# Causal attention in fp32 by row groups, four heads at a time, in a block of state-space scan, attention and experts

## What is computed

```
h   = layernorm(x, ln1_g, ln1_b)
qkv = (h @ Wqkv).reshape(B, T, 16, 48)
q, k, v = qkv[..., :16], qkv[..., 16:32], qkv[..., 32:]
q, k = rope(q), rope(k)                      # T = 2048
scores = einsum("bqhd,bkhd->bhqk", q, k) / sqrt(16)
scores = where(causal, scores, -1e9)
attn = einsum("bhqk,bkhd->bqhd", softmax(scores), v).reshape(B, T, 256) @ Wproj
x = x + attn                                 # then layernorm, gates, experts
```

## Time and profile before

| | us |
|---|---|
| median of three runs | 4523.81 |
| lowest and highest | 4516.04, 4532.55 |
| the profiled execution | 4527.28 |
| its span, first to last instruction | 4525.8 |
| PE busy | 3529.3 (78%) |
| DVE busy | 2918.2 (64%) |
| ACT busy | 2646.1 (58%) |
| POOL busy | 1823.3 (40%) |

### The profile page before, as it was taken

The page is one execution under the profiler, slowest core; times in us unless marked ns, Lnnn a source line. Parts: engine busy times, 40 slices in busy tenths (PEclk is TensorE's granted clock), DMA queues, the critical chain, the costliest instruction groups (busy, mean ns, idle before and its releaser), DMA issues. The chain is left out here.

```text
span 4525.8 us, 71351 instructions
## 1 busy us (share of the span) xinstructions
PE 3529.3 (78%) x20742; PEld 2162.1 (48%) x20742; DVE 2918.2 (64%) x4398; ACT 2646.1 (58%) x4174; POOL 1823.3 (40%) x1644
## 2 busy tenths in 40 slices
PE   8478788878878877847776888888888884599990
...
GB/s 204 133 107 91 85 96 100 97 85 95 85 87 99 89 93 85 85 133 198 177 164 87 25 27 25 24 20 25 27 25 27 25 12 140 102 77 77 66 29 186
DMA packets 183457, 385.83 MB, mean 85 GB/s; under 512 B 21763, under 2 KB 96630, under 8 KB 168624
## 3 DMA queue, kind: packets, MB, share of 16 engines
...
## 5 line engine op out<-in xcount | busy, mean ns | idle before, releaser
L506 POOL TENSOR_TENSOR scan_hC<-scan_hh,scan_cbc 128x512 f32<-128x512 f32 x1024 | 1383.2, 1379 | 159.0 <-DVE scan_hh L718 101.0
L718 DVE TENSOR_TENSOR_SCAN scan_hh<-scan_dA,scan_state,scan_bx 128x512 f32<-128x512 f32 x1024 | 1253.3, 1265 | 212.4 <-PE scan_bx L810 96.0
L1456 DVE TENSOR_REDUCE attend_mx<-attend_s 128x1 f32<-128x512 f32 (+1 forms) x1360 | 782.0, 608 | 342.1 <-PE attend_s L1586 222.1
L810 PE MATMUL scan_bx<-kept_ident,scan_dBxT 128*128 128x128 f32 x4096 | 675.8, 291 | 197.5 <-DVE scan_hh L718 133.7
L559 ACT ACTIVATE scan_dBxT<-scan_dtxT,scan_bt 128x512 f32<-128x512 f32 x1028 | 655.6, 710 | 81.5 <-PE scan_bx L810 81.3
L820 PE MATMUL scan_acc<-kept_ident,scan_hC 128*128 128x128 f32 x4128 | 655.7, 286 | 56.6 <-ACT scan_uu L568 29.9
L810 PEld LDWEIGHTS scan_bx<-kept_ident,scan_dBxT 128*128 128x128 f32 x4096 | 501.3, 150 | 389.1 <-DVE scan_hh L718 233.2
L554 ACT ACTIVATE scan_dA<-scan_dt,scan_an 128x512 f32<-128x512 f32 x1028 | 660.9, 712 | 29.4 <-DVE scan_hh L718 29.3
L1550 ACT ACTIVATE attend_full<-attend_s 128x1024 f32<-128x1024 f32 x384 | 392.0, 1025 | 332.2 <-PE attend_s L1613 328.2
L1586 PE MATMUL attend_s<-attend_kt,attend_qt 96*128 96x512 bf16 (+1 forms) x1360 | 482.8, 373 | 131.3 <-DVE attend_mx L1456 72.8
L820 PEld LDWEIGHTS scan_acc<-kept_ident,scan_hC 128*128 128x128 f32 x4128 | 516.3, 149 | 71.7 <-POOL scan_hC L506 38.3
...
...
## 6 DMA issues: line engine op xcount, KB each, us to landing
...
```

Source lines behind the costliest of these rows:

```text
L506: pool.tensor_tensor(hC[n % 2][:, m, :], h[:, m, :], rows, ALU.mult).then_inc(hc_ok, 1)
L718: dve.tensor_tensor_scan(hh[n % 2][:, m, r], dA[n % 2][:, m, r], bx[bank(j)][:, r], state[:, d, n, m:m + 1], ALU.mult, ALU.add).then_inc(h ...
L810: last = pe.transpose(bx[bank(j)][:, t * P:(t + 1) * P], dBxT[turned_slot(n)][:, t, m * P:(m + 1) * P], k["ident"][:, :])
L1456: dve.tensor_reduce(mx[:, t, c:c + 1], s1[v % 2][:, 0:w], AX_X, ALU.max).then_inc(s1_read, 1)
```

## The change

Queries and keys stay fp32 and are no longer split. In mix, POOL makes the rotation's sums, PE turns `rot` in four items of 128 columns (eight heads of q or of k), ACT copies four tiles of 512 columns and stores each. The reciprocal roots are issued in the third item and after the fourth.

```diff
-                        low(j - 1, q - 1)
-                low(JT - 1, t * JT + JT - 1)
+                    rotate(j, t * JT + j, t)
                 pool.wait_ge(v_out, t * JT + JT)
                 hold(pool, k)
                 pool.dma_start(vav[b, c].rearrange("p j (h e) -> p j h e", h=H), vt[i][:, :, :, :]
@@ -1086,12 +1076,6 @@
                 dve.tensor_tensor(ht[:, :, :], ht[:, :, :], gb[:, 1:2, :].broadcast_to([P, JT, D]), ALU.add
...
-                spread_parts(JT - 1, t * JT + JT - 1)
-                for h in range(H):
-                    g = h // 4
-                    act.wait_ge(hd_turned, t * H + h + 1)
-                    if h % 4 == 0:
...
+                for it in range(ITEMS):
+                    act.wait_ge(hd_turned, t * ITEMS + it + 1)
+                    act.wait_ge(stored_h[it], t * 16)
+                    act.activation(hd[it][:, :], ph[it % 2][:, :], ACT.Copy).then_inc(hd_out, 1)
+                    if it:
+                        store_heads(b, c, t, it - 1)
+                    if it == ITEMS - 2:
+                        rstd_of(0, t + 1)
+                store_heads(b, c, t, ITEMS - 1)
...
-                pe.wait_ge(lo_ok, t * JT + JT + 1)
-                for h in range(H):
-                    pe.wait_ge(hd_out, t * H + h)
-                    for w in range(2):
...
+                pe.wait_ge(rot_ok, t * JT + JT + 2)
+                for it in range(ITEMS):
+                    w, half = it // KD, it % KD
+                    pe.wait_ge(hd_out, t * ITEMS + it)
+                    for j in range(JT):
+                        last = pe.transpose(ph[it % 2][:, j * P:(j + 1) * P],
+                                            rot[:, j, w, half * (H // 2):(half + 1) * (H // 2), :].rearrange(
+                                                "p h e -> p (h e)"), k["ident"][:, :])
                     last.then_inc(hd_turned, 1)
```

```diff
+    HG = 4
+    GROUPS = B * H // HG
+    SETS = 3
+    PB = 3
+    HALF = C // 2
+    steps = [(qc, kt) for qc in range(NC) for kt in range(JT * qc + JT)]
+    NSTEP = len(steps)
+    N1 = HG * sum(t // JT + 1 for t in range(KT))
...
+    firsts = []
+    for t in range(KT - 1, -1, -1):
+        for c in range(t // JT + 1):
+            if t % JT == 0 and c == t // JT:
+                firsts[-1].append((t, c))
+            else:
+                firsts.append([(t, c)])
+    assert len(firsts) < NSTEP - 2
...
+            for n in range(GROUPS):
+                b, g = n // (H // HG), n % (H // HG)
+                for st, (qc, kt) in enumerate(steps):
+                    at = n * NSTEP + st
+                    if kt < JT * qc:
+                        continue
+                    o = (kt - JT * qc) * P
+                    pool.wait_ge(exp_ok, at * 2 + 2)
+                    own = pb[at % PB][:, :, o:o + P]
+                    pool.affine_select(out=own, in_=own, compare_op=ALU.is_ge, fill=0.0, base=0,
+                                       pattern=[[0, HG], [1, P]], channel_multiplier=-1).then_inc(kept_ok, 1)
+                    if st in ends:
+                        v = n * NC + qc
+                        pool.wait_ge(pv_out, v + 1)
+                        hold(pool, k)
...
+                for t, c, h in tiles1(st, (2, 3)) + tiles1(st, (0, 1)):
+                    bank = s1[v % S1]
+                    dve.wait_ge(s1_mm, v + 1)
+                    if c < t // JT:
+                        dve.tensor_reduce(mx[:, h, t, c:c + 1], bank[:, :], AX_X, ALU.max).then_inc(s1_read, 1)
+                    else:
+                        w = t % JT * P
+                        if w:
+                            dve.tensor_reduce(mx[:, h, t, c:c + 1], bank[:, 0:w], AX_X, ALU.max)
+                        if h == 2 and t < KT - 2:
+                            dve.wait_ge(edge_ok, n * KT + KT - 2 - t)
+                        dve.tensor_tensor(edge[t % 2][:, h, :], bank[:, w:w + P], cap_s[:, :], ALU.min
+                                          ).then_inc(s1_read, 1)
+                    v += 1
+                for t, c in firsts[st]:
+                    if c == t // JT:
+                        dve.wait_ge(s1_read, v)
+                        dve.tensor_reduce(mx[:, :, t, JT], edge[t % 2][:, :, :], AX_X, ALU.max).then_inc(edge_ok, 1)
...
+            for at in range(GROUPS * NSTEP):
+                qc, kt = steps[at % NSTEP]
+                o = max(kt - JT * qc, 0) * P
+                if at in outs:
+                    evacuate(outs[at])
+                if at >= PB:
+                    act.wait_ge(pv_ok, at - PB + 1)
+                for pair in range(2):
+                    act.wait_ge(s2_mm, at * 2 + pair + 1)
+                    own, score = pb[at % PB][:, 2 * pair:2 * pair + 2, :], s2[pair]
+                    if kt < JT * qc:
+                        act.activation(own, score[:, :, :], ACT.Exp).then_inc(exp_ok, 1)
                     else:
-                        for r in range(2):
-                            o = (2 * half + r) * P
-                            last = act.activation(buf[:, 2 * half + r, o:], s2[st % 2][:, r, o:], ACT.Exp)
-                    last.then_inc(s2_read, 1)
-                    if st - 2 in ends:
-                        evacuate(i, n, nth, ends.index(st - 2))
-                    if i == 1 and st - 1 in ADD_AT:
-                        invert(nth, ADD_AT[st - 1])
-                    if st == PLACE_AT:
-                        place_max((j + 2) % SETS, n + 2)
-                evacuate(i, n, nth, NC - 1)
-                if i == 1:
-                    invert(nth, NC - 1)
-            heads(act, head)
-            act.wait_ge(m_in, (B * H + 2) * 48)
+                        act.activation(below[pair][:, :, :], score[:, :, o:o + P], ACT.Relu, scale=-1.0
+                                       ).then_inc(clip_ok, 1)
+                        clips += 1
+                        if o + P < C:
+                            act.activation(own[:, :, o + P:], score[:, :, o + P:], ACT.Exp)
+                        act.wait_ge(clip_ok, clips)
+                        act.activation(own[:, :, o:o + P], below[pair][:, :, :], ACT.Exp, scale=-1.0
+                                       ).then_inc(exp_ok, 1)
+            evacuate(GROUPS * NC - 1)
...
+            def scores1(n, st, heads):
...
+                v = n * N1 + before1[st] + (0 if heads[0] == 2 else 2 * len(firsts[st]))
+                for t, c, h in tiles1(st, heads):
+                    rows = head_rows(h)
                     w = min(C, (t + 1) * P - c * C)
...
+                    if v >= S1:
+                        pe.wait_ge(s1_read, v - S1 + 1)
+                    pe.matmul(s1[v % S1][:, 0:w], qt[n % SETS][rows, t * P:(t + 1) * P],
+                              kt_[n % SETS][rows, c * C:c * C + w], start=True, stop=True).then_inc(s1_mm, 1)
+                    v += 1
...
+            def scores2(at, pair):
+                n, (qc, kt) = at // NSTEP, steps[at % NSTEP]
+                o = max(kt - JT * qc, 0) * P
+                if at % NSTEP == 0 and pair == 0:
+                    pe.wait_ge(m_in, (n + 1) * HG * 16)
+                if at:
+                    pe.wait_ge(exp_ok, at * 2 - 1 + pair)
...
+                    h = 2 * pair + i
+                    rows = slice(32 * h, 32 * h + ROWS)
+                    last = pe.matmul(s2[pair][:, i, o:], kt_[n % SETS][rows, kt * P:(kt + 1) * P],
+                                     qt[n % SETS][rows, qc * C + o:(qc + 1) * C], start=True, stop=True)
+                last.then_inc(s2_mm, 1)
...
+            def values(at, half):
+                n, (qc, kt) = at // NSTEP, steps[at % NSTEP]
+                b, g = n // (H // HG), n % (H // HG)
+                o = max(kt - JT * qc, 0) * P
+                if half == 0:
+                    pe.wait_ge(exp_ok, at * 2 + 2)
+                    if kt >= JT * qc:
+                        pe.wait_ge(kept_ok, n * KT + kt + 1)
+                    if kt == 0:
+                        pe.wait_ge(loaded_v[b], 16)
+                        if n * NC + qc:
+                            pe.wait_ge(pv_out, n * NC + qc)
+                lo, hi = max(o, half * HALF), (half + 1) * HALF
+                if lo >= hi:
+                    return
+                for h in range(HG):
+                    last = pe.matmul(pv[32 * h:32 * h + 32, lo:hi], vall[:, b * KT + kt, g * HG + h, :],
+                                     pb[at % PB][:, h, lo:hi], start=kt == 0 and half == 0,
+                                     stop=kt == JT * qc + JT - 1, skip_group_check=True)
+                if half == 1:
+                    last.then_inc(pv_ok, 1)
...
+            for at in range(GROUPS * NSTEP):
+                n, st = at // NSTEP, at % NSTEP
+                scores2(at, 0)
+                if n + 1 < GROUPS:
+                    scores1(n + 1, st, (2, 3))
+                if at:
+                    values(at - 1, 0)
+                scores2(at, 1)
+                if n + 1 < GROUPS:
```

(20 more changed lines are left out.)

504 lines of the change are left out of this document (154 added, 350 removed).

## The result

The changed kernel takes 5257.31 us (median of 4 runs, 5251.99 to 5260.87), the kernel before 4525.4 (4 runs): a ratio of 1.162, 95% interval 1.159 to 1.164. It is 732 us slower, where a time of 4320 us, 205 less than before, was forecast.

A forecast was written before the change was run, and what follows sets the result against it. PE, read in order by one queue, was taken to set the pace. From the profiled 4527.3 us, attend -187, mix -37 and route +16 gave 4319, stated as 4320 us; range 4220 to 4620, the forecast's own 4220 to 4420.

The forecast's parts named there:

- 111.8 us of PE per group: Attend, four heads: row phases 65.3, values 29.0 and 72 round trips 17.5 us, with columns at 2400 per us.
- rival 5: Attend: the clock stays at 1.2 GHz, 94 us more per group, less waits, +650: 4970 us; chance 0.05.
- the four row groups overlap fully: Attend: matmuls in four row groups run together, each row phase as long as its wider matmul; 65.3 us per group.
- rivals 1 and 4: Attend: 1, row groups' weight loads queue, 4620 us, chance 0.15; 4, row groups don't overlap in fp32, 5500 us, chance 0.05.
- Mix: Mix stage: shorter ring of PE, DVE and ACT work, -4.6 us in each of 8 chunks, -37 us.
- Attend's first record: Start of attend: first passes begin 12.5 us into the stage, where it was 19.
- the preface at DVE's pace: Attend's opening first passes: 104 us at DVE's pace, 133 with three banks at clock 0.50; 115 taken, plus 7 for maxima.
- The banks, 9 us per group: Attend: first-pass tiles wait for three banks, 0.13 us in each of 72 half steps, 9 us per group.
- the four steps with two first-pass tiles: Attend: steps with a second first-pass tile of 128 columns; only those columns were priced, 0.21 us.
- rival 2: Attend: a head's second-pass weights load in the open, 0.19 us per row phase, +120: 4440 us; chance 0.10.
- The triangle on POOL: Attend's diagonal steps: POOL clears the triangle of 4 x 128 elements, taken as 0.75 us.
- Route: Route stage: POOL's late product leaves 1.0 us per chunk, first two chunks without cover 8 us; +16 us in all.

The follow-up runs named there:

- rows32: The changed kernel with queries and keys read on all 32 rows of each row group, the added products being zero: 4649.19 us.
- before32: The kernel before, with only the first 32 of 96 (99) rows in both passes and the exponent scaled by 0.1: 5208.7 us.
- first32: Against rows32, 32 rows per head stay in the first pass only and the second pass has 17 again: 4815.26 us.
- fill: Against rows32, unused matmuls added in the two idle row groups during the last group of attend: 4565.15 us.
- kick: The changed kernel with 60 whole-array bf16 matmuls ahead of attend's preface and 60 ahead of its main part: 5264.25 us.
- heat: The changed kernel with one whole-array bf16 matmul of 512 columns added in each half step of attend: 5569.2 us.
- pre7: Against fill, seven banks instead of three for the first passes of the preface: 4526.03 us.
- narrow: Against rows32, DVE reduces 128 columns of each full first-pass tile and none left of the diagonal block, exponent scaled by 0.1: 4530.78 us.
- lag2: Against pre7, route's store of x before Ln and Exp, values two steps behind, four probability buffers, POOL's group-end store after next triangles: 4463.55 us.

## Why the prediction was wrong

**The step that failed** is the clock that the sum took for granted: 111.8 us of PE per group are columns at 2400 per us. The runs showed 1200 per us, a granted clock of 0.50 throughout attend, and groups of 242.2 us instead of 130. I gave the low clock 0.05 (rival 5) because "0.97 in the old main part with PE no busier" spoke against it. That compares busy time, and busy time was not what counted. What changed between the two kernels was the number of rows in the matmuls that fill PE's time: 96 or 99 before; 16 and 17 in each of four row groups after. rows32, before32, first32 and fill change the number of rows and little else, in both directions and in both kernels, and the clock follows each time. kick and heat, which add whole-array work instead, don't change it for longer than some 10 us. Why the chip grants less for fewer rows no run shows. Nothing in the rows of before warned of it: the preface at 0.50 had matmuls of 96 rows and PE busy for 44 of 59 us, so rows don't explain that one.

The Trainium skill ("TensorE: Matmul & The Clock Gate", section "Part 1: The HAM clock gate", its table of two states) has 2.4 GHz for a busy engine and 1.2 GHz for an idle one. The trace doesn't agree with "busy" as the profile counts it: 98% busy for 1696 us at 0.50.

**Rival 5's own price**, 4970 us, was 287 short. It doubled the streaming of a group (94 us) in all eight and took 100 us off for waits. The seven groups were 242 us, not 224, since the gaps between kinds and passes were 0.48 us per half step and not 0.24 (127 us in all) and no wait was saved (100); the rest is the preface (29), route (20) and the last group (8).

**Right**, by its own steps: the four row groups overlap fully (rivals 1 and 4 fall: loads and matmuls of different row groups start within 20 ns, and the passes are 1.02 us apart, one pass and a gap). Mix gave 33.5 us for 37. Attend's first record came 10.0 us sooner after mix for 6.5. The preface at DVE's pace, put at 104 us, is near what pre7 shows (99.8); at 1.2 GHz it took 151 with the turning and placing of maxima, where I took 122: the bound of 133 that I had worked out for three banks was nearer, and I should not have gone below it without a reason for a better clock.

The banks, 9 us per group, are borne out as far as narrow can tell (14 us with the clock's part, some 9 without).

**Right in kind, wrong in size:** the four steps with two first-pass tiles were priced by their columns alone; they cost some 7 us per group more, for want of a fourth bank. (The prediction counts 24 of 40 second-pass blocks as full. It is 28, as the first block on each diagonal has 512 columns too; the sum of 65.3 us is right for 28.) The second fp32 pass of a row group comes 0.10 to 0.11 us late; rival 2 had 0.19 for it and 0.10 as its chance, and the truth lies between it and the forecast's nothing, some 8 us per group. By the rule of the Trainium skill that I cited there (same page, section "The mechanism": loads overlap only in other row groups) that load would wait for the pass. The trace agrees by half: the load is recorded under the running pass of its own row group (3103.69, the pass from 3103.52), but the next pass doesn't follow without a gap. What makes the gap is not shown; a load that is partly in the open is one way. The triangle on POOL was put at 0.75 us and is 0.635. Route is +36 us instead of +16: 3.0 us a chunk instead of 1.0, since the Ln and Exp were followed to POOL and PE but not to the store behind them in ACT's own queue, and about 10 instead of 8 us at its start.

If the clock had been granted, the forecast would still have been too low: rows32 stands at 4649 us, and lag2, the best of the kernels run, at 4464. At full clock a group of four heads keeps PE for 94 us of streaming and 26 of gaps (0.36 us in 72 half steps), 120 in all by estimate, where it was 123 before; some 16 us go to having only three banks, 7 of them in the steps with a second tile. Masks and additions are gone, but gaps have come in their place.
